# Recurrent attention stage: the queries' rotated halves go to TensorE unsummed, the keys are summed on VectorE, and the stage's steps stand in another order

## The chip, the cores and the metric

The program runs on one core of a Trainium2 chip. The metric is device time in microseconds (us) for one execution of the whole program; lower is better. Three runs of the kernel before gave 5869.11, 5871.00 and 5874.72 us, median 5871.0.

## What is computed

The reference is a decoder of four layers in float32 over x of 16 sequences, 128 positions and 256 features. Each layer has attention, a second attention and a feed-forward part. The change lies in the first part alone, a delta-rule recurrence with 8 heads of 64 and 8 modes per head. In short, for each sequence and head:

```
q, k = l2norm(x Wq), l2norm(x Wk);  v = x Wv;  beta, decay, gate from x
for each of 8 modes m: rotate q and k by the position times the mode's frequency
    rot(y) = y * cos + swap(y) * sin          (swap: the halves of 64 exchanged, one negated)
    S_t = decay_t * S_(t-1) + beta_t * k_t (v_t - k_t^T S_(t-1))      out_t += weight_m * q_t^T S_t
y = (gate * out) Wo;  x = layernorm(x + y)
```

## The kernel before, in words

`delta_stage` (L581) takes the 16 sequences one after the other. The recurrence over 128 positions is written in blocks of Q = 32: decayed products of keys with keys (they couple positions) and of keys with queries (they read the result out), the inverse of the coupling inside each block, and a solve over the four blocks. The 64 chains (8 heads by 8 modes) are cut in two halves of 32, and each half in four **packs** (2 heads by 4 modes). Partitions hold 4 modes by 32 positions.

Work by engine, in the order in which each engine takes it:

- VectorE. `rotate` (L1093) makes for a pack the two products of `rot` for the keys (j = 0) and for the queries (j = 1): `plain` (L1102) into `kq`, `swapped` (L1107) into `t1`, 128x512 each. `evacuate` (L1112) multiplies the pack's products in PSUM by the decays: two instructions for key by key (L1119), two for key by query (L1124). `invert` (L1128) inverts 32x32 triangles of all lanes with 60 instructions that each wait for the one before (L1150, L1151); it puts steps of `rotate` between them. `gated` (L1157), `sum_squares`, `clip`, `normalise` (L1178) and the layer norm serve the start of the next sequence and the end of the last.
- GpSimd. `add_halves` (L674, L679) adds `t1` to `kq`, 128x512, for keys and for queries, so twice per pack. `roots` (L668, L672) raises the sums of squares to the power -0.5, and `stage_x` copies x.
- TensorE. `prepare` (L794): two matmuls (L798) spread the log decays of the pack, then 64 small ones (L809) make both kinds of products, keys and queries of a block in turn. They wait for both sums of the pack (`rotated`) and for PSUM to be free (`outputs_ready`). `solve` (L814) does the couplings (L828, L834), the blocks' solutions (L847) and the readout (L857). `carrier` (L724) is a 1-column matmul that carries a wait.
- ScalarE. `exponentials` (L972, L977) turns log decays into decays, `diagonal` (L981, L985) copies the diagonal blocks for `invert`, and `solve` (L989) copies between the steps.

One turn of the loop (L896, L1253) is `part_b(g)` and `part_a(g + 1)`. **Part b** on TensorE is `solve` of half 0 and the four packs of half 0 of the next sequence. **Part a** is `solve` of half 1, pack 0 of half 1, `finish` (L865), `values` (L742, L790), pack 1, `pre_a` (x of the next sequence turned and projected, L750, L742), packs 2 and 3, and `pre_b` (the normalised keys and queries turned, L761, and swapped, L766; then the decays' tables, L770 to L781). VectorE's `part_a` (L1189) inverts half 0 and evacuates half 1; `part_b` (L1214) the other way round. Order and waits are all written by hand.

Of the kernel before, what the change touches and what calls it, by code (L numbers as in the profile page):

```python
# [21 lines left out]
ALU = mybir.AluOpType  # L22
# [558 lines left out]
def delta_stage(k):  # L581
# [18 lines left out]
    consts_ready tables_ready angles_ready reduced halves_ready rotated products_ready blocks_ready outputs_ready  # L600
# [50 lines left out]
    with nc.Block() as block:  # L651
# [6 lines left out]
        def _(pool):  # L658
# [15 lines left out]
            def add_halves(u, p):  # L674
                n = u * PACKS + p
                for j in range(2):
                    pool.wait_ge(s["halves_ready"], n * 2 + j + 1)
                    both = kq[:, p % 2, :, j, :]
                    pool.tensor_tensor(both, both, t1[:, j, :, :], ALU.add).then_inc(s["rotated"], 1)  # L679

            def part_a(g, first, more, more2):
                u = g * 2 + 1
                add_halves(u, 0)
                add_halves(u, 1)
                add_halves(u, 2)
                if not first:
                    norm.roots(pool, g - 1)
                if more:
                    roots(g + 1)
                if more2:  # L690
                    pool.wait_ge(s["low_written"], at_A(g) + 7)
                    stage_x(g + 2)
                add_halves(u, 3)

            def part_b(g):
                for p in range(PACKS):
                    add_halves(g * 2 + 2, p)
# [6 lines left out]
            for p in range(PACKS):  # L704
                add_halves(0, p)
            part_a(0, True, True, True)
            with pool.Fori(0, B - 3) as g:
                part_b(g)
                part_a(g + 1, False, True, True)
            part_b(B - 3)  # L710
            part_a(B - 2, False, True, False)
            part_b(B - 2)
# [4 lines left out]
        def _(pe):  # L717
# [38 lines left out]
            def pre_b(g, low):  # L756
# [7 lines left out]
                for j in range(2):  # L764
                    bank = low.bank()
                    nc.tensor.matmul(ps[:, bank, :], w.swap, qkT[:, j, :, :], start=True, stop=True  # L766
                                     ).then_inc(s["low_written"], 1)
                pe.wait_ge(s["logs_ready"], g + 1)
# [25 lines left out]
            def prepare(u, hf, p, low):  # L794
# [6 lines left out]
                if not (isinstance(n, int) and n < 1):  # L801
                    pe.wait_ge(s["outputs_ready"], n * 2)
                carrier(2)
                for q in range(NQ):
                    for j in range(2):
                        for m in range(4):
                            for hh in range(2):
                                rows = slice(hh * DK, (hh + 1) * DK)
                                mm = nc.tensor.matmul(ps[m * Q:(m + 1) * Q, 2 + 2 * hh + j, AT[q]:AT[q] + P - q * Q],  # L809
                                                      kq[rows, p % 2, m, 0, q * Q:(q + 1) * Q],  # L810
                                                      kq[rows, p % 2, m, j, q * Q:P], start=True, stop=True)
                mm.then_inc(s["products_ready"], 1)
# [55 lines left out]
            def part_a(g, first, more):  # L868
# [23 lines left out]
            pre_b(0, low)  # L892
# [13 lines left out]
        def _(act):  # L906
# [40 lines left out]
            def pre_b(g, low, diagonal=None):  # L947
                act.wait_ge(s["decays_clipped"], g + 1)
                nc.scalar.activation(logs, logs, ACT.Ln).then_inc(s["logs_ready"], 1)
                if not (isinstance(g, int) and g < 1):  # L950
                    act.wait_ge(s["halves_ready"], g * (HALVES * PACKS * 2))
# [4 lines left out]
                if diagonal:  # L956
                    diagonal()
# [2354 lines left out]
```

## Time and profile before

| | us |
|---|---|
| median of three runs | 5871.0 |
| the profiled execution, its own time | 5864.7 |
| its span, first to last instruction | 5862.8 |
| GpSimd's sums L679 (256), busy | 373.7 |
| VectorE's inverse L1150, busy | 381.3 |
| TensorE's products L809 (16384 matmul records), busy | 280.4 |

The clock granted to TensorE over the whole span is 0.791 of full speed. One record of the profile is one pass of a matmul, so a float32 matmul of L809 has two records; each record has a weight load beside it (PEld). "issue" as the reason of an idle time means that the engine waited for nothing that the profile shows. An instruction's duration goes on while it waits for a port.

### The profile page before, as it was taken

The page shows a single profiled execution, that of the slowest core. Times are in us where ns is not written, and L with a number is a line of the kernel's source. Part 1 is how long each engine was busy: PE and PEld are TensorE (multiplying, and loading weights), DVE is VectorE, ACT ScalarE, POOL GpSimd, SP SyncE. Part 2 cuts the span into 40 slices and gives each one's busy share as a digit, 9 for nine tenths or more (in the row PEclk, how much of TensorE's full clock was granted, in tenths as well). Part 3 has the DMA queues.
Part 4 walks back from the last instruction along what each step waited for, and adds up shares of the span by engine and source line. Part 5 has one row for each costly group of instructions (what it writes and reads, how often), then busy time and mean ns, then how long its engine had stood idle before and what let it go on. Part 6 is the DMA issues. An engine that isn't in the chain of part 4 may idle for free. (4 is left out here: it accounts for less than half of the span.)

```text
span 5862.8 us, 127205 instructions
## 1 busy us (share of the span) xinstructions
PE 4132.5 (70%) x52916; PEld 2838.7 (48%) x52916; DVE 3427.7 (58%) x7691; ACT 1529.9 (26%) x3081; POOL 985.0 (17%) x753
## 2 busy tenths in 40 slices
PE   2677777767777775667878646766854777877897
PEld 1455555555555543555555423434632455655454
DVE  6778777777877743115454556882445454444445
ACT  2333333333333311112222231111333222321111
POOL 1222221222221222113222100001100121211000
PEclk8788888788878887888887765556866887888999
DMA  0000000000000001640000000001000000000000
GB/s 36 3 3 3 3 3 3 3 3 3 3 3 3 3 23 37 231 170 9 0 29 11 15 0 4 1 1 40 0 6 0 10 0 25 7 1 6 14 19 25
DMA packets 26763, 111.26 MB, mean 19 GB/s; under 512 B 2407, under 2 KB 15742, under 8 KB 22270
## 3 DMA queue, kind: packets, MB, share of 16 engines
q1 hardware_dynamic: 24702, 99.57, 4.8%
q8 instruction: 390, 6.39, 0.4%
q0 software_dynamic: 1536, 4.20, 0.2%
q14 instruction: 135, 1.11, 0.1%
HBM read 93.53 MB, written 10.22 MB: 18 GB/s over the span
## 5 line engine op out<-in xcount | busy, mean ns | idle before, releaser
L679 POOL TENSOR_TENSOR arena<-arena 128x512 f32<-128x512 f32 x256 | 373.7, 1462 | 1296.8 <-DVE arena L1107 1296.8
L1150 DVE TENSOR_TENSOR arena<-weights,arena 128x30 f32<-128x30 f32 (+14 forms) x960 | 381.3, 397 | 33.2 <-DVE arena L1151 3.3
L144 POOL TENSOR_TENSOR arena<-arena,eps 128x4 f32<-128x4 f32 (+2 forms) x76 | 15.1, 199 | 2186.6 <-DVE arena L139 2186.6
L422 PE MATMUL psum<-ident,arena 128*128 128x128 f32 x1280 | 217.6, 325 | 212.6 <-ACT arena L493 212.6
L402 PE MATMUL psum<-arena 128*128 128x512 f32 x640 | 353.4, 685 | 16.8 <-ACT arena L482 11.2
L1151 DVE TENSOR_TENSOR arena<-arena 128x30 f32<-128x30 f32 (+14 forms) x960 | 317.6, 331 | 30.3
L414 PEld LDWEIGHTS psum<-arena 128*128 128x128 f32 x2048 | 280.8, 214 | 100.8 <-issue 59.7
L809 PE MATMUL psum<-arena 64*32 64x128 f32 (+2 forms) x16384 | 280.4, 286 | 50.5 <-issue 50.5
L300 POOL TENSOR_TENSOR arena<-arena,weights 128x1024 f32<-128x1024 f32 x128 | 242.5, 1902 | 405.1 <-PE psum L402 339.1
L977 ACT ACTIVATE arena<-psum,arena 128x128 f32<-128x128 f32 (+3 forms) x1024 | 240.2, 340 | 249.9 <-PE psum L798 246.7
L414 PE MATMUL psum<-arena 128*128 128x17 f32 x2048 | 272.9, 277 | 33.4 <-ACT arena L490 33.4
L1398 PE MATMUL psum<-arena 128*128 128x512 f32 x576 | 260.6, 598 | 50.5 <-DVE Y L1462 35.8
L422 PEld LDWEIGHTS psum<-ident,arena 128*128 128x128 f32 x1280 | 178.8, 171 | 234.8 <-ACT arena L493 234.6
L809 PEld LDWEIGHTS psum<-arena 64*32 64x32 f32 x16384 | 258.7, 126 | 61.3 <-issue 60.6
L724 PE MATMUL psum<-arena 128*128 128x1 bf16 x400 | 71.6, 179 | 281.8 <-ACT arena L993 98.9
L493 ACT ACTIVATE arena<-arena 128x1024 f32<-128x1024 f32 x160 | 169.7, 1061 | 349.4 <-DVE arena L549 348.3
L553 DVE RECIPROCAL arena<-psum 128x16 f32<-128x16 f32 x80 | 20.6, 258 | 384.1 <-PE psum L414 384.1
L1107 DVE TENSOR_TENSOR arena<-arena,Y 128x512 f32<-128x512 f32 x256 | 244.4, 955 | 0.0
L1119 DVE TENSOR_TENSOR arena<-psum,arena 128x320 f32<-128x320 f32 x256 | 113.6, 481 | 222.8 <-PE psum L809 219.1
L798 PE MATMUL psum<-arena 96*128 96x320 f32 x512 | 212.0, 529 | 44.7 <-ACT arena L970 21.6
L490 ACT COPY arena<-psum 128x1024 f32<-128x1024 f32 x160 | 162.1, 1013 | 307.8 <-PE psum L422 307.8
L724 PEld LDWEIGHTS psum<-arena 128*128 128x128 bf16 x400 | 40.5, 101 | 413.7 <-ACT arena L993 156.0
(457 smaller groups left out, 8678.5 us busy)
## 6 DMA issues: line engine op xcount, KB each, us to landing
arena<-in_experts_L_ffn SPq DMA_DIRECT2D x23, 2052.0 KB
arena<-in_ctxT SPq DMA_DIRECT2D x16, 512.0 KB, 3.4
arena<-in_experts_L_ffn SPq DMA_DIRECT2D x18, 384.0 KB, 3.0
weights<-in_w_L_ffn SPq DMA_DIRECT2D x1, 3072.0 KB, 9.9
weights<-in_w_L_attn SPq DMA_DIRECT2D x1, 2960.5 KB, 13.0
routed_x<-arena SPq DMA_DIRECT2D x1, 2944.0 KB, 16.5
routed_y<-arena SPq DMA_DIRECT2D x23, 128.0 KB, 1.7
weights<-in_w_L_ffn SPq DMA_DIRECT2D x1, 2753.0 KB, 10.2
```

What stands on the lines that cost most here:

```text
L300: pool.tensor_tensor(km[:, j % 2, :, :], bc(keys, 1, HH), bc(w.heads, 2, P), ALU.mult).then_inc(keys_spread, 1)
L402: mm = nc.tensor.matmul(out[:, b * 4:b * 4 + 4, :], qT[:, c, u * P:(u + 1) * P], km[:, at % 2, b * 4:b * 4 + 4, :], start=True, stop=True)
L414: mm = nc.tensor.matmul(o_psum[:, c * HH + h, :], pT[:, j % 2, h, :], v, start=True, stop=True)
L422: mm = nc.tensor.transpose(pt_psum[:, h, :], pr[:, j % 2, h, :], k.ident[:, :])
L679: pool.tensor_tensor(both, both, t1[:, j, :, :], ALU.add).then_inc(s["rotated"], 1)
L798: nc.tensor.matmul(ps[:, bank, 0:SPAN], pick[0:CHAINS + Q, hf * SLOTS + slot(p, hh), :], moving[0:CHAINS + Q, :], start=True, stop=True).t ...
L809: mm = nc.tensor.matmul(ps[m * Q:(m + 1) * Q, 2 + 2 * hh + j, AT[q]:AT[q] + P - q * Q], kq[rows, p % 2, m, 0, q * Q:(q + 1) * Q], kq[rows, ...
L977: a = nc.scalar.activation(LA[hf][:, t, 1, run], ps[:, bank, run], ACT.Exp, bias=bias[:, hf * SLOTS + t, q:q + 1])
L1107: dve.tensor_tensor(t1[:, j, :, :], bc(qkS[:, j, c, :], 1, 4), sin[:, c, modes4, :], ALU.mult).then_inc(s["halves_ready"], 1)
L1150: linked(dve.tensor_tensor(part, bc(lanes[:, j + 1:, j], 2, j), bc(inv[:, j, 0:j], 1, below), ALU.mult))
L1151: linked(dve.tensor_tensor(inv[:, j + 1:, 0:j], inv[:, j + 1:, 0:j], part, ALU.add))
L1398: mm = nc.tensor.matmul(ps[:, bank, :], W[s][name][:, c, f * P:(f + 1) * P], xT[:, g, c, :], start=(c == 0), stop=(c == C - 1))
```

## The change

The order on VectorE and TensorE, word for word from the built programs. The first place is one pack in the loop on TensorE, `prepare`. Before:

```order
L798 MATMUL psum<-arena 128x320
L800 ISA
L802 REGISTER_ALU
L724 MATMUL psum<-arena 128x1
L809 MATMUL psum<-arena 32x128 x16
L809 MATMUL psum<-arena 32x96 x16
L809 MATMUL psum<-arena 32x64 x16
L809 MATMUL psum<-arena 32x32 x16
```

The same place on TensorE in the change (L779 is L798 of before, L703 the carrier, L792 the products):

```order
L703 MATMUL psum<-arena 128x1
L792 MATMUL psum<-arena 32x128 x8
L792 MATMUL psum<-arena 32x96 x8
L792 MATMUL psum<-arena 32x64 x8
L792 MATMUL psum<-arena 32x32 x8
L784 REGISTER_ALU
L703 MATMUL psum<-arena 128x1
L792 MATMUL psum<-arena 32x128 x16
L792 MATMUL psum<-arena 32x96 x16
L792 MATMUL psum<-arena 32x64 x16
L792 MATMUL psum<-arena 32x32 x16
```

A pack has now 32 products of keys and then 64 of queries, with a second carrier between them: 96 in place of 64.

The second place is TensorE's part a, behind the projections of `values`. Before:

```order
L790 MATMUL psum<-arena,weights 128x128 x8
L735 REGISTER_ALU
L798 MATMUL psum<-arena 128x320
L735 REGISTER_ALU
L798 MATMUL psum<-arena 128x320
L800 ISA
L724 MATMUL psum<-arena 128x1
L809 MATMUL psum<-arena 32x128 x16
```

In the change, at the same place on TensorE (L771 is L790, L729 is L750, L721 is L742):

```order
L771 MATMUL psum<-arena,weights 128x128 x8
L726 REGISTER_ALU
L714 REGISTER_ALU
L729 MATMUL psum<-ident,arena 128x128 x2
L731 REGISTER_ALU
L714 REGISTER_ALU
L721 MATMUL psum<-weights,arena 128x512 x4
L714 REGISTER_ALU
L721 MATMUL psum<-weights,arena 128x128 x2
L714 REGISTER_ALU
L779 MATMUL psum<-arena 128x320
```

The next sequence's x is turned and projected ahead of pack 1. In the same way the turns and swaps (L761, L766; now L740, L745) stand ahead of pack 3, and only the tables behind it.

The third place is VectorE's `rotate` of one pack in the loop's part a. Before:

```order
L1102 TENSOR_TENSOR arena<-arena,weights 128x4x128
L1106 ISA
L1107 TENSOR_TENSOR arena<-arena,Y 128x512
L1102 TENSOR_TENSOR arena<-arena,weights 128x4x128
L1106 REGISTER_ALU
L1107 TENSOR_TENSOR arena<-arena,Y 128x512
```

In the change, at the same place on VectorE:

```order
L1120 TENSOR_TENSOR arena<-psum,arena 128x2x320
L1125 SCALAR_TENSOR_TENSOR arena<-psum,arena 128x320 x2
L1091 TENSOR_TENSOR arena<-arena,weights 128x4x128
L1095 ISA
L1096 TENSOR_TENSOR arena<-arena,Y 128x512
L1100 TENSOR_TENSOR arena<-arena,weights 128x4x128
L1103 REGISTER_ALU
L1104 TENSOR_TENSOR arena<-arena 128x4x128
L1108 TENSOR_TENSOR arena<-arena,Y 128x4x128
```

Five steps in place of four: L1104 sums the keys' halves, and the queries' swapped half (L1108) goes into `kq` of its own. The evacuation ahead of it is one instruction for both heads' keys (L1120) and two for the queries.

The core of the diff:

```
-    kq = A(2, 4, 2, P)
-    t1 = A(2, 4, P)
+    kq = A(2, 4, 3, P)
+    t1 = A(4, P)
...
-    inv, prod = A(Q, Q), A(Q * Q // 4)
+    prod = A(Q * Q // 4)
...
-            def add_halves(u, p):
-                n = u * PACKS + p
-                for j in range(2):
-                    pool.wait_ge(s["halves_ready"], n * 2 + j + 1)
-                    both = kq[:, p % 2, :, j, :]
-                    pool.tensor_tensor(both, both, t1[:, j, :, :], ALU.add).then_inc(s["rotated"], 1)
...
                 pe.wait_ge(s["rotated"], (n + 1) * 2)
...
+                for j, free, ready in ((0, "blocks_ready", "keys_ready"), (1, "outputs_ready", "queries_ready")):
+                    if not (isinstance(n, int) and n < 1):
+                        pe.wait_ge(s[free], n * 2 if j else n)
+                    carrier(2 + 2 * j)
+                    parts = (1, 2) if j else (0,)
+                    for q in range(NQ):
+                        for part in parts:
...
+                                                          kq[rows, p % 2, m, part, q * Q:P],
+                                                          start=(part == parts[0]), stop=(part == parts[-1]))
+                    mm.then_inc(s[ready], 1)
...
                 values(low)
-                prepare(u, 1, 1, low)
                 if more:
                     pre_a(g + 1, low)
+                prepare(u, 1, 1, low)
                 prepare(u, 1, 2, low)
+                if more:
+                    turns(g + 1, low)
                 prepare(u, 1, 3, low)
                 if more:
-                    pre_b(g + 1, low)
+                    tables(g + 1, low)
...
                 diagonal(u, 1, 0)
+                diagonal(u, 1, 1)
                 if more:
-                    pre_b(g + 1, low, lambda: diagonal(u, 1, 1))
-                else:
-                    diagonal(u, 1, 1)
+                    tables(g + 1, low)
...
+                def summed():
+                    dve.wait_ge(s["halves_ready"], n + 1)
+                    dve.tensor_tensor(kq[:, p % 2, :, 0, :], kq[:, p % 2, :, 0, :], t1[:, :, :], ALU.add
+                                      ).then_inc(s["rotated"], 1)
+
+                def swapped_queries():
+                    dve.tensor_tensor(kq[:, p % 2, :, 2, :], bc(qkS[:, 1, c, :], 1, 4), sin[:, c, modes4, :], ALU.mult
+                                      ).then_inc(s["rotated"], 1)
+
+                return [keys, swapped_keys, queries, summed, swapped_queries]
...
+                pair = L.rearrange("p (c h a) j t -> p c h a j t", c=2, h=2)[:, p // 2, :, p % 2, :, :]
+                kk = ps[:, 2:4, 0:SPAN]
+                dve.tensor_tensor(pair[:, :, 0, :], kk, pair[:, :, 1, :], ALU.mult).then_inc(s["blocks_ready"], 1)
...
-                linked(dve.tensor_copy(inv[:, :, :], lanes[:, :, :]))
-                linked(dve.memset(flat(inv)[:, 0:Q * Q:Q + 1], 1.0))
+                linked(dve.memset(flat(lanes)[:, 0:Q * Q:Q + 1], 1.0))
```

GpSimd's `add_halves` is gone with all its calls. The inverse is made in place in `lanes`, without the copy L1144. VectorE's `part_a` evacuates pack 1 behind `sum_squares` and `clip`, and runs `normalise` ahead of the evacuation of pack 2 and of the norm's last step.

## Rows read from the trace of the kernel before

**Rows 1.** Groups of instructions of the stage, 60 to 2060 us (count, busy, mean ns, idle before).

```profile
L679 POOL TENSOR_TENSOR arena<-arena 128x512 f32<-128x512 f32 x256 | 373.7, 1462 | 1296.8 <-DVE arena L1107 1296.8
...
L1107 DVE TENSOR_TENSOR arena<-arena,Y 128x512 f32<-128x512 f32 x256 | 244.4, 955 | 0.0
...
L1102 DVE TENSOR_TENSOR arena<-arena,weights 128x512 f32<-128x512 f32 x256 | 208.4, 814 | 5.4 <-ACT arena L955 5.4
...
L1178 DVE SCALAR_TENSOR_TENSOR arena<-arena 128x512 f32<-128x512 f32 x32 | 47.6, 1526 | 5.1 <-POOL arena L672 3.3
...
L1144 DVE COPY arena<-weights 128x1024 f32<-128x1024 f32 x32 | 22.0, 687 | 0.6
```

**Rows 2.** Windows of one turn: length, busy of PE, PEld, DVE, ACT, POOL; granted clock.

```profile
938.14:972.28 34.14, 26.19 (x854) 19.44 (x855) 32.09 (x72) 7.88 (x19) 5.66 (x4) 0.85 0.02 4
972.28:996.38 24.10, 14.74 (x467) 10.46 (x468) 17.86 (x30) 9.12 (x36) 7.47 (x5) 0.85 0.01 3
996.38:1026.68 30.30, 20.57 (x786) 15.61 (x784) 27.98 (x69) 5.42 (x15) 4.19 (x3) 0.89 0.02 4
1026.68:1064.36 37.68, 29.53 (x520) 20.38 (x520) 19.54 (x37) 20.64 (x51) 10.76 (x9) 0.77 0.01 2
```

**Rows 3.** Timeline of VectorE in both inversions: start, us, line, idle before and its end.

```profile
938.14 1.25 DVE L1143 STREAM_TRANSPOSE weights<-weights 128x1024 f32<-128x1024 f32 x1 [3.72 <-ACT weights L985]
...
946.02 1.77 DVE L1102 TENSOR_TENSOR arena<-arena,weights 128x512 f32<-128x512 f32 x1
...
1000.10 1.25 DVE L1150 TENSOR_TENSOR arena<-weights,arena 128x30 f32<-128x30 f32 x1
```

**Rows 4.** One line's instructions in the same turn: ns min/median/max, first and last start.

```profile
L1107 DVE TENSOR_TENSOR arena<-arena,Y x16: 675/682/1755, 942.5 to 1050.5; 128x512 f32<-128x512 f32 x16
```

**Rows 5.** Timeline of TensorE, end of part b's solve and its packs.

```profile
959.44 0.87 PE L828 MATMUL psum<-arena 32*32 32x64 f32 x47 [0.54 <-issue]
...
963.32 0.94 PE L847 MATMUL psum<-arena,weights 32*32 32x64 f32 x50 [0.64 <-issue]
...
965.06 4.28 PE L857 MATMUL psum<-arena 128*64 128x128 f32 x64
...
974.84 1.66 PE L809 MATMUL psum<-arena 64*32 64x128 f32 x127
978.77 0.19 PE L809 MATMUL psum<-arena 64*32 64x32 f32 x1 [2.27 <-issue]
...
981.15 2.22 PE L809 MATMUL psum<-arena 64*32 64x128 f32 x120
984.69 0.27 PE L809 MATMUL psum<-arena 64*32 64x32 f32 x8 [1.32 <-issue]
...
990.71 0.29 PE L809 MATMUL psum<-arena 64*32 64x32 f32 x15 [2.06 <-issue]
```

**Rows 6.** The page, DMA queues: packets, MB, share.

```profile
q8 instruction: 390, 6.39, 0.4%
```

**Rows 7.** Timeline of TensorE in part a behind `gated`, one turn earlier.

```profile
900.91 3.51 PE L865 MATMUL psum<-weights,arena 128*128 128x256 f32 x8 [6.97 <-DVE arena L1159]
...
907.75 0.70 PE L798 MATMUL psum<-arena 96*128 96x320 f32 x2
...
910.70 2.50 PE L809 MATMUL psum<-arena 64*32 64x128 f32 x128
...
914.35 4.14 PE L742 MATMUL psum<-weights,arena 128*128 128x512 f32 x12 [0.54 <-ACT arena L939]
...
921.94 2.58 PE L809 MATMUL psum<-arena 64*32 64x128 f32 x128
...
929.80 0.18 PE L724 MATMUL psum<-arena 128*128 128x1 bf16 x1 [4.01 <-POOL arena L679]
...
932.42 1.97 PE L761 MATMUL psum<-ident,arena 128*128 128x128 f32 x8
934.21 2.22 PE L766 MATMUL psum<-arena,weights 128*128 128x512 f32 x4
```

More of the change, by code:

```diff
@@ L690, in part_a @@
                 if more2:
-                    pool.wait_ge(s["low_written"], at_A(g) + 7)
+                    pool.wait_ge(s["low_written"], at_A(g) + 5)
                     stage_x(g + 2)
[L693 to L697, printed above, removed]
             pool.wait_ge(s["consts_ready"], 1)
@@ L800, in prepare @@
                 pe.wait_ge(s["rotated"], (n + 1) * 2)
[L801 to L812, printed above, removed]
+                for j, free, ready in ((0, "blocks_ready", "keys_ready"), (1, "outputs_ready", "queries_ready")):
[5 more added lines that the diff above has]
+                        for part in parts:
+                            for m in range(4):
+                                for hh in range(2):
+                                    rows = slice(hh * DK, (hh + 1) * DK)
+                                    mm = nc.tensor.matmul(ps[m * Q:(m + 1) * Q, 2 + 2 * j + hh,
+                                                             AT[q]:AT[q] + P - q * Q],
+                                                          kq[rows, p % 2, m, 0, q * Q:(q + 1) * Q],
+                                                          kq[rows, p % 2, m, part, q * Q:P],
+                                                          start=(part == parts[0]), stop=(part == parts[-1]))
+                    mm.then_inc(s[ready], 1)
             def solve(g, hf):
@@ L891, in _ @@
             pre_a(0, low)
-            pre_b(0, low)
+            turns(0, low)
+            tables(0, low)
             for p in range(PACKS):
@@ L1026, in _ @@
             pre_a(0, low)
-            pre_b(0, low)
+            turns(0, low)
+            tables(0, low)
             for p in range(PACKS):
@@ L1110, in rotate, with keys, swapped_keys @@
-                return steps
+                def keys():
+                    if turned is not None:
+                        dve.wait_ge(s["low_taken"], turned)
+                    dve.tensor_tensor(kq[:, p % 2, :, 0, :], bc(qkT[:, 0, c, :], 1, 4), cos[:, c, modes4, :], ALU.mult)
+                def swapped_keys():
+                    if not (isinstance(n, int) and n < 1):
+                        dve.wait_ge(s["rotated"], n * 2 - 1)
+                    dve.tensor_tensor(t1[:, :, :], bc(qkS[:, 0, c, :], 1, 4), sin[:, c, modes4, :], ALU.mult
+                                      ).then_inc(s["halves_ready"], 1)
@@ L1149, in invert @@
                     part = prod[:, 0:below * j].rearrange("p (a b) -> p a b", b=j)
[L1150 to L1151 removed]
+                    linked(dve.tensor_tensor(part, bc(lanes[:, j + 1:, j], 2, j), bc(lanes[:, j, 0:j], 1, below), ALU.mult))
+                    linked(dve.tensor_tensor(lanes[:, j + 1:, 0:j], lanes[:, j + 1:, 0:j], part, ALU.add))
                 assert not between
```

82 lines of the change are left out of this document (30 added, 52 removed).

## The prediction

> **What bounds the kernel now.** I read the groups of instructions of the stage first. GpSimd's 256 sums (L679) take 1.46 us each and VectorE's instructions beside them are long: L1107 has a mean of 0.955 us, L1102 of 0.814 [rows 1]. Then one line alone: of 16 L1107 in a turn the median is 0.682 us and the longest 1.755 [rows 4]. So most run at 0.68 and some at 1.75, and the timeline shows these where a sum of GpSimd runs: 1.77 us for an L1102, 1.25 for an L1150 of 30 columns that elsewhere takes 0.2 [rows 3]. A collision costs VectorE about 1.07 us.
>
> Next the windows of one turn, cut where VectorE changes work: inversion of part b to `gated` (34.14 us), evacuation of part b (24.10), inversion of part a (30.30), evacuation of part a (37.68), together 126.2 us [rows 2]. VectorE is busy for 94% and 92% of the inversions, but for 74% and 52% of the evacuations. There it waits for TensorE. The change touches this stage alone, so I count one turn, and 15.5 of them (16 sequences, with a short first and last).
>
> Last, why TensorE is late in part b. Its packs stop in the middle of a run of equal matmuls, with "issue" as the reason: 2.27, 1.32 and 2.06 us [rows 5]. Between two such stops lie always 126 records: 1 + 4 (L798) + 1 (carrier) + 120, then 8 + 4 + 1 + 113. A record has a weight load, so that is 252 instructions, and the page has a queue that brings instructions in packets of 6.39 MB / 390 = 16.4 KB [rows 6]. I read it so: TensorE runs out of instructions and waits for the next packet. Where nothing else holds it up, packets are 963.32 - 959.44 = 3.9 us apart; in the packs, with a wait for VectorE between them, 5.9 and 6.0 us [rows 5]. A packet's records need only 126 x 13.1 ns = 1.7 us (1.66 us for 127) [rows 5].
>
> **The change part by part**, per turn.
>
> *GpSimd's sums go.* VectorE's collisions go with them. In the inversion of part b four instructions are of the long kind (one stands in [rows 3]): -4.3. In that of part a two of L1150: -2.1. In the evacuations some more, beside waits, L1178 among them (mean 1.526 against 0.68) [rows 1].
>
> *The sum comes to VectorE.* Eight packs, a fifth 128x512 instruction each. Started back to back, one takes some 0.6 us of VectorE (0.68 less the overlap): two more steps in the inversion of part b, +1.2, one in that of part a, +0.6, five in the evacuations, +3.0, the most of it under waits for TensorE.
>
> *The copy L1144 goes*, twice 0.69 [rows 1]: -0.7 in each inversion. One evacuation of 640 columns for two of 320, the memset and the order of `clip` and `sum_squares` I cost at nothing: they move 0.1 us and stand before waits.
>
> *Inversion of part a*: -2.1 - 0.7 + 0.6 = -2.2. VectorE is the bound here, TensorE waits 6.97 us at its end [rows 7].
>
> *Inversion of part b*: VectorE alone would save 4.3 + 0.7 - 1.2 = 3.8. But `gated` needs TensorE's readout, L857, which ends at 965.06 + 4.28 = 969.34, 2.9 before `gated` at 972.28 [rows 2, 5]. And the solve starts later against the inversion: the tables (1.3 us) now stand behind pack 3, and then come the loop's jump and the solve. I take -1.5, between -2.9 and 0.
>
> *Packs of part b.* Now 192 records, 4 of L798 and 2 carriers: 198, four times 792, that is 6.3 packets. One is there: 1.7 us; the other 5.3 take 3.9 each, 20.6. Last product 22.3 us after the readout, where before it was 991.0 - 972.3 = 18.7 after `gated`: +3.6. Behind it VectorE's next rotation has no collision but a fifth step, -1.1 + 0.6, and pack 0's part of the work had lain before `gated` (nearly 3 us of it; that is why the gap between readout and `gated` is spent first): of these I leave -0.8. So part b together: -1.5 + 3.6 - 0.5 - 0.8 = +0.8. Price of a packet between 1.7 (hidden) and 5.9; I take 3.9, the row with nothing else in it, since the new second wait (keys free PSUM ahead of queries) lets TensorE run on.
>
> *Evacuation of part a* is a chain over TensorE, which I put together anew from [rows 7]: from `gated` 0.5; `finish` and `values`, 900.91 to 907.75, 6.8; x turned and copied, 913.20 to 914.35, 1.2; projections, ScalarE's part and the decays, 914.35 to 921.94, 7.6; packs 1 and 2 with 192 records between 13.1 and 20.2 ns (2.58 us for 128), 2.5 to 3.9, I take 3.2 each; decays between them 1.4; turns and swaps, 932.42 to 936.4, with ScalarE 4.3; decays 1.4; pack 3 3.2 and its evacuation 1.0. Sum 33.8. Gone are the 4.01 us in which pack 3 waited for GpSimd's sum [rows 7] and the 3.72 in which the inversion waited for ScalarE's diagonals behind the turns [rows 3]. Packets: three packs are 4.7 of them, some 2.7 of which can't be there in time; I add 2.0. So 35.8 against 37.68 [rows 2]: -1.9, bounds -3.9 (all there) and +1.5 (5.9 us each). And L865 ran 3.51 us for 8 records of 256, the lower level of the clock (1.2 GHz), behind its 6.97 us of waiting [rows 7]; its wait shrinks by the 2.2 of the inversion and the 1.0 of the longer pack 0. Half of 1.7 us: -0.8.
>
> **Sum**: +0.8 - 2.2 - 1.9 - 0.8 = -4.1 us per turn, times 15.5 is -64 us. The profiled execution took 5864.7 us; the median of the runs, 5871.0, is 6 above. So 5801 on its clock and **5807** as a median.
>
> **A rule of the Trainium skill against the row.** The row shows stops of 2.27, 1.32 and 2.06 us, 126 records apart [rows 5]. In "Runtime: NRT & Kernel Launch", section on instruction fetch mechanics, the Trainium skill says that the sequencer fetches the next 16 KiB page while it works on the current one, and that crossing the boundary is "mostly hidden". By that rule the added instructions would cost their execution alone, the first rival below; the trace disagrees, since what stops the packs comes at just this spacing.
>
> **The rivals.**
>
> *The added packets are hidden* (chance 0.10). Then part b follows VectorE and the readout: -2.9, the packs nothing; part a -2.2 - 3.9. Together -9.0, 5731 us. For it: no such stops stand in part a's rows [rows 7]. Against it: part b's three.
>
> *TensorE's instructions become the bound* (0.12, slower). Place: the packs, 5.3 packets beyond the first in part b and 2.7 in part a, 8.0 together. Each 1 us above 3.9 adds 8.0 us, so from 4.4 us per packet the gain is gone. Half way to the 5.9 seen between the stops of part b, 4.9 us, the turn is 8.0 - 4.1 = 3.9 longer: 5931. For it: each pack still waits for VectorE in two places. Against it: the 3.9 of the solve, where TensorE waits for ScalarE as well.
>
> *Nothing is left* (0.08, within 0.2%). The solve of part b starts 4 us later against the inversion than before (tables, then the jump, L834), VectorE waits at `gated` for it, and -1.5 becomes +2.6: 5871.
>
> *The change doesn't do what it says*: the order shows 96 products per pack and no sum on GpSimd, so I give it nothing.
>
> **The numbers.** The forecast has 0.70; with the first rival 0.80 is faster by over 0.2% (12 us, about what a measurement of this kernel tells from no change), 0.08 within it, 0.12 slower. The range holds the forecast's own bounds, the hidden packets below and the zero case's near side above: 5735 to 5868. Left out are the slower rival and a part of the zero case.
>
> **What would show it.** VectorE's 128x512 instructions all near 0.68 us; windows of 28 us for part a's inversion and some 35 for its evacuation; part b as long as before, with two stops "issue" per pack or so, 126 records apart, near 2 us each; q8 with about 64 packets more (128 packs x 128 instructions more / 252). The forecast is wrong if part b grows by over 4 us, if part a's packs show stops above 2 us each, or if VectorE waits over 3 us at `gated` in part b.

## The result and the profile after

Four executions of the changed kernel gave 5778.6 to 5792.0 us, median **5778.9**; four of the kernel before, in the same comparison, had a median of 5872.9. The ratio is 0.9845, with a 95% interval of 0.9828 to 0.9862: 94 us less. The forecast was 5807 us, 64 less, within 5735 to 5868.

| | before | after |
|---|---|---|
| span of the profiled execution | 5862.8 | 5776.9 |
| GpSimd busy, whole span | 985.0 | 602.4 |
| VectorE busy, whole span | 3427.7 | 3284.6 |
| TensorE's products, stops "issue" before them (groups) | 50.5 | 119.7 |
| clock granted to TensorE, share of full speed | 0.791 | 0.819 |

The groups of instructions after, 60 to 1975 us, which answer to [rows 1] (count, busy, mean ns, idle before with its end):

```profile
L792 PE MATMUL psum<-arena 64*32 64x128 f32 (+3 forms) x24576 | 375.8, 243 | 120.5 <-issue 119.7
...
L1125 DVE SCALAR_TENSOR_TENSOR arena<-psum,arena 128x320 f32<-128x320 f32 x256 | 129.2, 546 | 124.2 <-PE psum L792 118.6
...
L1120 DVE TENSOR_TENSOR arena<-psum,arena 128x640 f32<-128x640 f32 x128 | 105.0, 820 | 144.5 <-ACT arena L965 109.6 <-PE psum L792 33.1
...
L1100 DVE TENSOR_TENSOR arena<-arena,weights 128x512 f32<-128x512 f32 x128 | 87.8, 686 | 0.0
L1108 DVE TENSOR_TENSOR arena<-arena,Y 128x512 f32<-128x512 f32 x128 | 87.7, 685 | 0.0
...
L1178 DVE SCALAR_TENSOR_TENSOR arena<-arena 128x512 f32<-128x512 f32 x32 | 20.6, 684 | 3.3 <-POOL arena L672 3.3
```

The 128x512 instructions have now one length, 0.68 to 0.69 us, where L1107 had a mean of 0.955 and L1178 of 1.526. What VectorE waits for stands in the other rows: TensorE's queries (118.6 us) and ScalarE's decays (109.6).

The windows of one turn, cut at the same places as [rows 2]:

```profile
893.47:924.39 30.92, 22.80 (x721) 16.93 (x722) 28.30 (x73) 4.78 (x9) 0.00 (x0) 0.83 0.02 4
924.39:949.68 25.29, 19.66 (x860) 15.41 (x861) 16.52 (x28) 11.85 (x43) 0.00 (x0) 0.96 0.02 5
949.68:977.44 27.76, 21.07 (x851) 15.88 (x849) 25.54 (x69) 5.49 (x15) 0.00 (x0) 0.97 0.02 4
977.44:1016.15 38.71, 30.69 (x715) 20.43 (x715) 17.82 (x35) 18.10 (x49) 4.24 (x5) 0.91 0.01 3
```

Both inversions are shorter. The evacuation of part b is longer, that of part a no shorter. One turn can stand 2 us off another, so the table below has means: the same four pieces, taken from the starts of the inversion's first transpose (L1143, now L1144) and of `gated` (L1159 in both) in each trace, over the 14 turns between the second sequence and the last.

| run | median us | inversion b | evacuation b | inversion a | evacuation a | turn |
|---|---|---|---|---|---|---|
| before | 5872.9 | 34.1 | 23.3 | 30.3 | 37.8 | 125.4 |
| **after** | 5778.9 | 30.2 | 25.3 | 27.8 | 37.4 | 120.7 |
| e1_products_64 | 5753.2 | 31.9 | 21.9 | 27.8 | 37.2 | 118.8 |
| e2_products_128 | 5996.8 | 30.4 | 33.9 | 27.8 | 42.2 | 134.1 |
| e11_narrow_products | 6000.2 | 30.8 | 34.1 | 27.8 | 41.6 | 134.3 |
| e3_old_order | 5794.2 | 30.8 | 26.2 | 27.8 | 36.5 | 121.2 |
| e4_before_no_sums | 5742.4 | 30.4 | 24.2 | 28.0 | 35.5 | 118.1 |
| e5_keys_on_gpsimd | 5821.8 | 31.5 | 25.0 | 28.2 | 38.0 | 122.7 |
| e6_queries_on_vector | 5821.0 | 32.1 | 24.1 | 28.1 | 38.2 | 122.5 |
| e7_before_in_place | 5857.3 | 33.4 | 23.8 | 29.4 | 38.0 | 124.6 |
| e8_late_queries | 5734.1 | 32.2 | 22.7 | 28.4 | 34.2 | 117.5 |
| e9_values_first | 5685.2 | 30.4 | 25.4 | 27.8 | 30.6 | 114.2 |
| e10_both | 5672.3 | 32.1 | 22.7 | 28.4 | 30.2 | 113.3 |
| e12_unrolled | 5669.4 | 31.7 | 22.1 | 28.4 | 31.5 | 113.7 |

One execution of e11_narrow_products took 14692.5 us at a granted clock of 0.572 and bears on no reading; without it that run's median is 5999.4 us.

A turn is 4.7 us shorter. Fourteen of them are 65.7 us, but the distance from the first inversion to the last shrank by 86.6 (1928.8 to 1842.2). Most of the rest lies in the first turn, which took 119.3 us and takes 100.3. Its part a has no `solve` and no `finish`. The first turn's windows before, from one inversion's first transpose to the next, columns as above:

```profile
123.83:185.17 61.34, 30.02 (x642) 19.88 (x643) 44.95 (x100) 20.60 (x51) 14.64 (x10) 0.68 0.00 1
185.17:243.15 57.98, 41.86 (x1320) 31.26 (x1321) 49.84 (x101) 17.08 (x53) 13.16 (x9) 0.72 0.01 3
```

and after:

```profile
123.95:172.67 48.72, 29.26 (x834) 21.34 (x834) 41.54 (x97) 16.65 (x47) 3.61 (x3) 0.81 0.01 2
172.67:224.28 51.61, 39.95 (x1646) 30.16 (x1646) 44.57 (x102) 17.85 (x54) 0.00 (x0) 0.97 0.02 4
```

Part b's packs on TensorE after, which answer to [rows 5] (start, us, line, idle before and its end):

```profile
930.72 0.28 PE L792 MATMUL psum<-arena 64*32 64x32 f32 x10 [0.44 <-issue]
930.93 0.18 PE L703 MATMUL psum<-arena 128*128 128x1 bf16 x1
931.04 1.53 PE L792 MATMUL psum<-arena 64*32 64x128 f32 x117
934.20 0.28 PE L792 MATMUL psum<-arena 64*32 64x32 f32 x11 [1.62 <-issue]
...
938.03 1.06 PE L792 MATMUL psum<-arena 64*32 64x96 f32 x83 [0.51 <-issue]
...
941.51 0.39 PE L792 MATMUL psum<-arena 64*32 64x64 f32 x26 [0.47 <-issue]
...
945.26 0.34 PE L792 MATMUL psum<-arena 64*32 64x32 f32 x27 [1.90 <-issue]
```

Between two stops lie 126 to 128 records (10 + 1 + 117 in the first gap). The stops are 3.48, 3.83, 3.48 and 3.75 us apart, 3.6 on average, where before they were 5.9 and 6.0. The packs now run at about the pace that the solve had shown (3.9). The page counts 454 packets of instructions for 390 [rows 6]:

```profile
q8 instruction: 454, 7.44, 0.5%
```

### The profile page after: what moved, and what is told of

Same layout as the page of the kernel before. It is cut to its first block and busy times, and to the rows that moved or that the text cites. A ratio compares the mean times of both kernels' runs of the same rounds, so it can differ in the third digit from the quotient of the medians.

```text
span 5776.9 us, 143172 instructions
## 1 busy us (share of the span) xinstructions
PE 4179.0 (72%) x61228; PEld 2889.5 (50%) x61236; DVE 3284.6 (57%) x7659; ACT 1490.3 (26%) x3051; POOL 602.4 (10%) x497
## 5 line engine op out<-in xcount | busy, mean ns | idle before, releaser
L792 PE MATMUL psum<-arena 64*32 64x128 f32 (+3 forms) x24576 | 375.8, 243 | 120.5 <-issue 119.7
L792 PEld LDWEIGHTS psum<-arena 64*32 64x32 f32 x24576 | 323.2, 108 | 180.8 <-issue 178.2
L402 PE MATMUL psum<-arena 128*128 128x512 f32 x640 | 356.2, 690 | 16.8 <-ACT arena L482 11.2
L1151 DVE TENSOR_TENSOR weights<-weights,arena 128x30 f32<-128x30 f32 (+14 forms) x960 | 318.0, 331 | 32.1 <-DVE arena L1150 2.9
L1150 DVE TENSOR_TENSOR arena<-weights 128x30 f32<-128x30 f32 (+14 forms) x960 | 317.7, 331 | 29.3
L414 PEld LDWEIGHTS psum<-arena 128*128 128x128 f32 x2048 | 282.9, 216 | 101.7 <-issue 60.9
L414 PE MATMUL psum<-arena 128*128 128x17 f32 x2048 | 274.8, 278 | 33.4 <-ACT arena L490 33.4
L1398 PE MATMUL psum<-arena 128*128 128x512 f32 x576 | 260.6, 598 | 50.5 <-DVE Y L1462 35.8
L813 PEld LDWEIGHTS psum<-arena 32*32 32x32 f32 x12288 | 188.1, 108 | 87.3 <-issue 85.9
L813 PE MATMUL psum<-arena 32*32 32x64 f32 x12288 | 219.0, 220 | 12.0 <-issue 11.6
L819 PE MATMUL psum<-arena 128*128 128x512 f32 x256 | 182.4, 801 | 50.0 <-issue 47.3
L402 PEld LDWEIGHTS psum<-arena 128*128 128x128 f32 x640 | 133.0, 227 | 136.8 <-issue 110.7
L1125 DVE SCALAR_TENSOR_TENSOR arena<-psum,arena 128x320 f32<-128x320 f32 x256 | 129.2, 546 | 124.2 <-PE psum L792 118.6
L1398 PEld LDWEIGHTS psum<-arena 128*128 128x128 f32 x576 | 109.5, 191 | 165.6 <-issue 109.0
```

The costliest lines, as they stand in the source:

```text
L402: mm = nc.tensor.matmul(out[:, b * 4:b * 4 + 4, :], qT[:, c, u * P:(u + 1) * P], km[:, at % 2, b * 4:b * 4 + 4, :], start=True, stop=True)
L414: mm = nc.tensor.matmul(o_psum[:, c * HH + h, :], pT[:, j % 2, h, :], v, start=True, stop=True)
L792: mm = nc.tensor.matmul(ps[m * Q:(m + 1) * Q, 2 + 2 * j + hh, AT[q]:AT[q] + P - q * Q], kq[rows, p % 2, m, 0, q * Q:(q + 1) * Q], kq[rows, ...
L813: mm = nc.tensor.matmul(ps[rows, 6, t * DK:(t + 1) * DK], Lu[rows, t, 0, col:col + Q], Wn[rows, t, by, :], start=False, stop=(by == q - 1 ...
L819: mm = nc.tensor.matmul(ps[:, 6, :], repeat[:, q, :], bc(slots, 2, 2), start=True, stop=(q == 0))
L1150: linked(dve.tensor_tensor(part, bc(lanes[:, j + 1:, j], 2, j), bc(lanes[:, j, 0:j], 1, below), ALU.mult))
```

## The experiments

In what was expected, theory P is that of the prediction: packets of instructions set the length of part b's packs.

**What a product costs, by itself and by its instructions.** Three runs with 64, 128 and again 128 products per pack, the last with added products of 8 columns in place of 32 to 128. The edits, each to the change:

```
e1: -  parts = (1, 2) if j else (0,)      +  parts = (1,) if j else (0,)
e2: -  parts = (1, 2) if j else (0,)      +  parts = (1, 2, 2) if j else (0,)
e11:   as e2, the added product with q * Q:q * Q + 8 in place of q * Q:P
```

> The change with the queries' second product left out of TensorE (64 products per pack again, 32 fewer); the result leaves out sin * swap(q), VectorE still makes it. Theory P (packets of instructions set the length of part b's packs, 3.9 us per 126 records): 64 records fewer are half a packet, 2.0 us per pack, of which part b gives back some 5 of 8 before VectorE binds and part a some 3: about -8 us per turn, 5655 us; q8 back to about 390 packets. Rival X (only their execution counts, 13.1 ns a record): 0.84 us per pack, -3.4 in part b and at most -2.5 in part a: 5690 to 5730 us. Rival V (VectorE hides them): under -1 us per turn, 5765 or more.

> The change with the queries' second product made twice, so 128 products per pack, 64 records more per pack (the result has that half twice). Theory P: +2.0 us per pack in part b and +1 to +2 in three packs of part a: +11 to +13 us per turn, 5950 to 5980 us, with stops 'issue' in the packs summing to more than twice those of the change (120 us before L792) and about 64 packets more in q8. Rival X: the records' execution alone, +0.84 us per pack, +3.4 and +2.5 per turn: 5870 us. Rival V: under +1 us per turn, 5795 or less.

> As the run with 128 products per pack (5996.8 us), but the 32 added products of each pack are 8 columns wide in place of 128 to 32, so they bring the same number of instructions and nearly no work (the result has sin * swap(q) twice in 8 of a block's columns). Theory P (the count of instructions, by their packets, is what costs): the evacuation of part b stays near 33.9 us as with the wide ones (33 to 34), q8 near 519 packets, 5960 to 5995 us. Rival X (the products' own execution and the clock): most of the 218 us that the wide ones cost goes away, the evacuation of part b near 26 to 28 us, 5800 to 5860 us.

Measured: 5753.2, 5996.8 and 6000.2 us, against 5778.9 for the change. The 32 products that the change adds cost 26 us, the next 32 cost 218, and 32 of 8 columns cost 221. The window of one evacuation of part b with the wide ones:

```profile
878.78:912.62 33.84, 24.84 (x1103) 19.36 (x1105) 16.48 (x29) 11.10 (x42) 0.00 (x0) 0.84 0.02 4
```

the same with the narrow ones:

```profile
1019.46:1054.15 34.69, 25.14 (x1099) 19.61 (x1102) 16.48 (x29) 11.31 (x42) 0.00 (x0) 0.82 0.02 4
```

the page's queue with the narrow ones (the wide ones have the same 519):

```profile
q8 instruction: 519, 8.50, 0.6%
```

and TensorE's timeline with the narrow ones:

```profile
1022.94 1.47 PE L793 MATMUL psum<-arena 64*32 64x96 f32 x128 [0.42 <-issue]
1026.69 0.25 PE L793 MATMUL psum<-arena 64*32 64x32 f32 x3 [2.27 <-issue]
...
1045.95 1.59 PE L793 MATMUL psum<-arena 64*32 64x128 f32 x128 [0.49 <-issue]
1049.70 0.45 PE L793 MATMUL psum<-arena 64*32 64x8 f32 x27 [2.15 <-issue]
```

with the wide ones, from the same place as the third of these lines:

```profile
1038.53 1.61 PE L792 MATMUL psum<-arena 64*32 64x128 f32 x128 [0.48 <-issue]
```

As many added instructions with a small part of the columns cost the same: what is paid for is the count. The narrow run alone does not tell packets from execution, since a narrow record takes TensorE nearly as long: 128 records, a third of them narrow, take 1.59 us and 128 wide ones 1.61, and the window has 25.14 us busy for 24.84. Two other numbers do. The 64 added records cost 2.1 us per pack in part b (8.5 over four), where theory P had 2.0 and their execution at 13.1 ns is 0.84. And the stops with the narrow ones are 3.75 us and 128 records apart at a granted clock of 0.82, hardly more than in the change at 0.96, so the lower clock explains little of it. The runs lie 17 and 5 us above theory P's ranges, and its size is right for these 64 records.

It is not right for the 64 records that the change itself adds. There part b's evacuation grew by 3.4, or 0.85 per pack, which is their execution, and part b's inversion gave 1.7 of it back. With 64 products VectorE waits at `gated` for the readout (L1159, 32 of them):

```profile
L1159 DVE TENSOR_TENSOR arena<-psum,arena 128x256 f32<-128x256 f32 x32 | 13.2, 414 | 49.1 <-PE psum L842 49.1
```

Of the 49.1 us, 25.3 stand before the last `gated` of the program, which has such a wait in every run; the rest is 1.5 us in nearly every turn. The change has 0.9 us in all before its first 30. TensorE's solve starts 6.3 us behind the inversion's first transpose, where in the change it is 3.4 (means of the 14 turns). So the next solve came too late for the shorter packs to be worth their full length. Of the three theories for that run none had the time: X came nearest from one side (5690 to 5730), V from the other (5765 or more).

**What the sums on GpSimd cost.** The kernel before, its sums cut to one column:

```
-                    both = kq[:, p % 2, :, j, :]
-                    pool.tensor_tensor(both, both, t1[:, j, :, :], ALU.add)
+                    both = kq[:, p % 2, 0:1, j, 0:1]
+                    pool.tensor_tensor(both, both, t1[:, j, 0:1, 0:1], ALU.add)
```

> The kernel before with GpSimd's sums cut from 128x512 to one column, so that the sum of the halves is left out of the result but for that column; all waits and the order as before. Theory C (a sum of GpSimd makes the VectorE instruction beside it 1.07 us longer): all 128x512 instructions of L1102 and L1107 near 0.68 us, inversion of part b -2.9 to -4.3, inversion of part a -2.1, evacuation of part a -3 to -4 with the wait for L679 gone, of part b -1: 9 to 11 us per turn, 5700 to 5730 us. Rival N (the long instructions have another cause, such as the order or PSUM): the long ones stay near 1.75 us, only the wait of 4.01 us goes, 5810 us.

And the change with the keys' sum given back to GpSimd (`summed` leaves VectorE's list, GpSimd has `add_halves` again for j = 0):

> The change with the keys' sum back on GpSimd (128 sums in place of 256), the queries unsummed on TensorE as in the change; VectorE has four steps per pack. Theory C: each of the eight sums per turn falls on a VectorE instruction and makes it 1.07 us longer, where VectorE's own step would take 0.60: in the inversions, three sums, +0.5 each, +1.4; in the evacuations the sum also comes later to TensorE (1.46 + 0.3 us behind the last step, against 0.68), +1 per pack that TensorE waits for, 2 to 3 of them: +3 to +5 us per turn, 5825 to 5855 us. Rival L (one step less on VectorE outweighs it): 5740 to 5770 us.

Measured: 5742.4 us, 133 below the 5875.2 of the kernel before in the same comparison, and 5821.8, 43 above the change. One line's instructions in the first of the two (ns min/median/max):

```profile
L1107 DVE TENSOR_TENSOR arena<-arena,Y x256: 675/687/708, 93.6 to 1921.4; 128x512 f32<-128x512 f32 x128
```

and in the second, with GpSimd's sum:

```profile
L1122 DVE TENSOR_TENSOR arena<-arena,Y x128: 677/1755/1775, 94.6 to 1996.1; 128x512 f32<-128x512 f32 x128
...
L678 POOL TENSOR_TENSOR arena<-arena x128: 1284/1653/3710, 94.2 to 1995.6; 128x512 f32<-128x512 f32 x128
```

Without the sums no instruction of L1107 is longer than 0.71 us, where [rows 4] had 1.755. With one sum per pack 1.755 is the median of the line beside it. Theory C stands: the collision is the cause, 1.07 us each. The sums of the expectations were too high: 133 us and 7.3 per turn for 9 to 11 (part b's evacuation gave nothing), and 43 us and 2.0 per turn for 3 to 5. The Trainium skill says in "SBUF — State Buffer", section "Who interferes with whom", that a VectorE instruction with two SBUF inputs contends with a GpSimd instruction that reads SBUF; these three rows agree.

**What one step on VectorE costs.** The change with the queries summed on VectorE too, so six steps and 64 products:

```
-                return [keys, swapped_keys, queries, summed, swapped_queries]
+                return [keys, swapped_keys, queries, summed, swapped_queries, summed_queries]
```

> The change with the queries' halves summed on VectorE too: six steps per pack, 64 products per pack on TensorE; the same result. Theory P (a pack's 32 added products cost up to 2.0 us of packets in part b, a VectorE step 0.60): part b's packs some 3 us shorter, the inversions 3 x 0.60 = 1.8 longer, part a's packs about 1 shorter: -2 us per turn, 5735 to 5760 us. Rival X (the products cost 0.84 us per pack and partly lie under VectorE's waits): the step costs more than it saves, +1 us or more per turn, 5790 to 5810 us.

Measured: 5821.0 us. Against the run with 64 products, which has one step fewer and the same products, that is 68 us for the sixth step: 3.7 per turn. Three of its eight stand in part b's evacuation and cost 2.1, two in part a's and cost 0.9, the one in part a's inversion costs 0.4 and the two in part b's 0.2, since with 64 products VectorE waits 1.5 us for the readout there and the added steps fill that wait. Rival X was right and still too low. A step costs its 0.60 us or more only in part b's evacuation (0.7).

**The copy and the order.** The kernel before with the inverse made in place alone (`inv` replaced by `lanes`, L1144 gone), and the change with part a's steps in the order of before:

> The kernel before with the inverse made in place, so the copy L1144 gone, and nothing else changed. By the prediction's step: -0.7 us in each inversion where VectorE is the bound, so -0.7 in part a and -0.7 in part b (the readout ends 2.9 us ahead of gated): -1.4 us per turn, 5850 us. Rival: the inversion's rotate steps then meet GpSimd's sums at other places and TensorE's next pack comes no earlier, so nothing: 5866 to 5873 us.

> The change's products and sums, but the steps of part a in the order of the kernel before (pack 1 ahead of the next x, turns and tables behind pack 3, diagonals of the second half behind the turns). Theory O (the new order is worth the 3.72 us in which the inversion waited for ScalarE's diagonals, and little else, since the 4.01 us of waiting for GpSimd's sum is gone in either order): +3 to +5 us per turn in part a, 5825 to 5855 us; part b as in the change. Rival C (all of the gain comes from VectorE's collisions with GpSimd, the order is worth nothing): 5770 to 5790 us. Rival G (the order is all of the gain): 5860 us or more.

Measured: 5857.3 us, 0.9969 of before (0.9957 to 0.9982), 18 us or 0.8 per turn in the means for the 1.4 of the expectation. The old order: 5794.2 us, 15 above the change. A steady turn is 0.5 us longer, from part b (+0.9 and +0.6 us); part a's evacuation is 0.9 *shorter* in the old order. That makes 7 us in 14 turns. Another 7.4 lie in the first turn (107.7 us for 100.3). The first transpose then waits for ScalarE's diagonals (59.3 us over 32), where in the change it waits 25.9 for "issue" alone. So theory O (+3 to +5 per turn) was wrong by a factor of six or more, and rival C nearly right: in the steady turns the order is worth half a microsecond, and in the first turn 7.4.

**Where VectorE waits in the change.** Its timeline in the turn shown above, the waits alone:

```profile
924.39 0.43 DVE L1159 TENSOR_TENSOR arena<-psum,arena 128x256 f32<-128x256 f32 x1 [0.65 <-PE psum L842]
...
945.75 1.01 DVE L1125 SCALAR_TENSOR_TENSOR arena<-psum,arena 128x320 f32<-128x320 f32 x2 [2.79 <-PE psum L792]
...
993.99 1.22 DVE L1164 TENSOR_REDUCE arena<-arena 128x16 f32<-128x1024 f32 x1 [10.24 <-ACT arena L931]
...
1013.14 1.01 DVE L1125 SCALAR_TENSOR_TENSOR arena<-psum,arena 128x320 f32<-128x320 f32 x2 [2.46 <-PE psum L792]
1016.15 1.25 DVE L1144 STREAM_TRANSPOSE weights<-weights 128x1024 f32<-128x1024 f32 x1 [2.00 <-issue]
```

Two of these kinds can be tried by a move alone. The 2.79 and 2.46 us are waits for the last pack's queries, which the inversion does not need:

```
-                    evacuate(u, 0, 3, e + 6)
+                    evacuate_keys(u, 0, 3, e + 6)
...
-                invert(g * 2, ch, rotate(u, 1, 1))
+                invert(g * 2, ch, [lambda: evacuate_queries(g * 2, 0, 3)] + rotate(u, 1, 1))
```

(and the same for the other half). The 10.24 us are the chain that begins at `gated`:

```
                 prepare(u, 1, 0, low)
+                values(low)
                 if not first:
                     finish(g - 1)
-                values(low)
```

> The change with one thing moved on VectorE: in the last pack of each half only the keys are evacuated ahead of the inversion (it needs nothing else), the queries' two instructions L1125 go behind the inversion's first transpose. Theory Q (the 2.8 and 2.5 us in which VectorE waits for the products of the last pack's queries stand on the path that sets the turn): -3 us in part b and -3 in part a, 6 us per turn, 5685 us, and the readout becomes what gated waits for. Rival R (TensorE's solve, which follows its own packs, tables and jump, sets gated anyway): gated waits for the readout, -1 us per turn or less, 5765 us.

> The change with values (the projections L721 and L771) ahead of finish on TensorE, in the time in which it waits for gated; nothing else moved. Theory S (part a's evacuation is a chain from gated over finish, values, the turned x and the projections, 977.88 to 993.97 in the trace of the change, and VectorE waits 10.24 us for its end): the 4.2 us of values leave the chain, and ScalarE's sigmoid with its table load starts with gated and not 7.3 us behind it: -4 to -6 us per turn, all in the evacuation of part a, 5690 to 5720 us. Rival P (behind that chain come the packs, whose packets then bind): -1 us per turn or less, 5765 us.

> Values ahead of finish and the last pack's queries evacuated behind the inversion's transpose, together. Theory: the two lie on different stretches (evacuation of part a; end of both evacuations), so they add: -3 for the late queries (measured alone) and -4 to -6: 5640 to 5680 us. Rival (the readout becomes the bound of both halves once VectorE comes earlier): less than the larger of the two alone, 5690 us or more.

Measured: 5734.1, 5685.2 and 5672.3 us. The late queries took 2.7 and 3.2 us from the two evacuations and gave 2.0 and 0.6 back to the inversions. Both inversions now hold the two moved instructions, and in part b's `gated` waits 1.2 us per turn for the readout besides: half of theory Q, half of rival R. Values ahead of `finish` took 6.8 us from part a's evacuation and moved no other piece by over 0.2, theory S and a little beyond its 4 to 6. The window of one evacuation of part a in that run:

```profile
941.27:972.32 31.05, 25.09 (x710) 17.59 (x708) 17.84 (x36) 18.11 (x49) 4.25 (x5) 1.00 0.01 3
```

and what is left in it of the wait of 10.24 us:

```profile
950.22 1.22 DVE L1164 TENSOR_REDUCE arena<-arena 128x16 f32<-128x1024 f32 x1 [2.63 <-ACT arena L931]
```

TensorE's clock, 0.91 in that window of the change, is 1.00: the engine now has `values` to do ahead of `gated`. Together they gave 13 us beyond the better one, against some 45 if they added. So 5672.3 lies within the 5640 to 5680 of the expectation and still the two do not add. The result, 0.9653 of the kernel before (0.9637 to 0.9669), computes the same function and is 107 us below the change.

**The jump of TensorE's loop.** The last run takes that kernel and writes the loop's body twice:

```
-            with pe.Fori(0, B - 2) as g:
-                part_b(g, True)
-                part_a(g + 1, False, True)
+            with pe.Fori(0, (B - 2) // 2) as h:
+                for g in (h * 2, h * 2 + 1):
+                    part_b(g, True)
+                    part_a(g + 1, False, True)
```

> Both rearrangements of the run before (5672.3 us) and TensorE's loop body written out twice, so that 7 jumps in place of 14 stand ahead of part b's first L819. Theory J (the stop of 3.5 us 'issue' there is the jump, and behind it the solve and the readout set gated in part b): half of the stops gone, the inversion of part b 1.5 us shorter on average, 5645 to 5655 us. Rival (instead of the jump a packet is waited for at the same place, since the two stops have one cause): 5668 to 5676 us.

Measured: 5669.4 us, 3 below, within what such a measurement can tell. The groups of the products and of the solve's first matmuls with the body written twice:

```profile
L792 PE MATMUL psum<-arena 64*32 64x64 f32 (+3 forms) x24576 | 378.1, 245 | 135.1 <-issue 134.6
L819 PE MATMUL psum<-arena 128*128 128x512 f32 x256 | 170.0, 751 | 24.5 <-issue 21.6 <-DVE arena L1167 2.8
```

and in the kernel that it was made from:

```profile
L792 PE MATMUL psum<-arena 64*32 64x128 f32 (+3 forms) x24576 | 377.1, 244 | 110.6 <-issue 109.5
L819 PE MATMUL psum<-arena 128*128 128x512 f32 x256 | 180.3, 793 | 50.5 <-issue 49.4 <-DVE arena L1166 1.0
```

The stops ahead of L819 fell by 27.8 us and those in the packs grew by 25.1. A stop of 3.4 to 4.0 us stands behind the loop's jump 13 times with the body written once and 6 times (3.3 to 3.8 us) with it written twice, as often as the loop jumps back. The rival had the time right. The Trainium skill, "Runtime: NRT & Kernel Launch", section on instruction fetch mechanics, says that a taken branch whose target is outside the current window of two pages causes an instruction-fetch stall, and that this is a reason to unroll. Here a stall at the jump is seen; that its cause is this fetch is not shown, and unrolling moved it without making the sum less.

## Why the prediction was right, and where it was not

*Collisions* (-4.3 and -2.1 in the inversions, priced at 1.07 each from [rows 3, 4]): right, by the run without sums and the run with one sum.

*Inversion of part a*, -2.2: measured -2.5, and about 28 us as said. VectorE is the bound there: 27.8 to 28.4 in every run without GpSimd's 256 sums, whatever TensorE does.

*Inversion of part b*, -1.5: measured -3.8. This is exactly what was worked out for VectorE alone (4.3 + 0.7 - 1.2). The step that failed is the cut from 3.8 to 1.5, the readout as the next bound. The first matmul of TensorE's solve, and the readout after, in the turns shown (938.14 and 893.47 are the inversion's first transpose):

```profile
941.40 1.96 PE L834 MATMUL psum<-arena 128*128 128x512 f32 x2 [3.44 <-issue]
```

```profile
897.15 2.07 PE L819 MATMUL psum<-arena 128*128 128x512 f32 x2 [3.89 <-issue]
...
920.07 4.28 PE L842 MATMUL psum<-arena 128*64 128x128 f32 x64
```

Two things were mis-sized. The 2.9 us between the readout and `gated` are those of one turn; over the 14 turns before they are 4.7 on average (2.8 to 9.6). And the solve was to start later against the inversion, but it starts 3.4 us behind the first transpose where it had been 3.2 (means), so the readout ends as early as before, 29.0 us behind the transpose for 29.4. The readout is the next bound, but just reached: in the change `gated` waits for it in two of its first 30 places, 0.65 us in the turn shown.

```profile
L1159 DVE TENSOR_TENSOR arena<-psum,arena 128x256 f32<-128x256 f32 x30 | 12.0, 400 | 0.9 <-PE psum L842 0.9
```

With 64 products (e1) and with the late queries (e8), where the inversion starts earlier against TensorE's solve, this piece grew back by 1.7 and 2.0.

*Packs of part b*, +3.6 with -0.5 and -0.8 behind it, so +2.3: measured +2.1. The size is right, and the stops "issue" are there, 126 to 128 records apart. In the turn shown the last product ends 21.2 us behind `gated`, where I had 22.3: the price of a packet was taken as 3.9 and is 3.6. There are five stops over the four packs and not two per pack, and they are shorter than the 2 us each that I expected, 0.44 to 1.90. That packets are the reason for the +2.1 itself is not shown: taking the 32 added products away again gave 0.85 us per pack, no more than their execution. The rule of the Trainium skill that crossing a page is mostly hidden would have made the packs cost their execution; but five stops stand in four packs of the turn shown, 4.9 us together, and 64 records beyond the change cost 2.1 us per pack for 0.84 of execution, so the measurement decides against it here.

*Evacuation of part a*, -1.9, and -0.8 for the clock: measured -0.4. This is the term that failed. TensorE's timeline of the turn after, in the places that my chain named:

```profile
977.88 3.22 PE L850 MATMUL psum<-weights,arena 128*128 128x256 f32 x8 [3.55 <-DVE arena L1159]
...
987.45 5.84 PE L721 MATMUL psum<-weights,arena 128*128 128x512 f32 x12 [2.17 <-ACT arena L927]
...
995.28 0.94 PE L792 MATMUL psum<-arena 64*32 64x128 f32 x64
...
1004.00 1.09 PE L740 MATMUL psum<-ident,arena 128*128 128x128 f32 x8 [0.95 <-DVE arena L1178]
```

The products of pack 1 start 17.8 us behind `gated` (977.44), where my chain had 0.5 + 6.8 + 1.2 + 7.6 = 16.1. Of the 1.7 between them ScalarE has 1.4: from the turned x (984.90) to its projections (987.45) it is 2.6 us for the 1.2. Its timeline there:

```profile
985.17 1.28 ACT L958 ACT_TABLE_LOAD   x1 [1.26 <-PE psum L771]
986.46 0.60 ACT L958 ACTIVATE arena<-psum 128x512 f32<-128x512 f32 x1
986.96 0.37 ACT L927 COPY arena<-psum 128x256 f32<-128x256 f32 x1
```

x's copy (L927) now stands directly behind the gate's sigmoid (L958) and its table load, and TensorE waits 2.17 us for it, where in [rows 7] it waited 0.54. And behind the last pack I had its evacuation as the end; in fact VectorE then stops 2.00 us at what must be its own loop's jump: such a stop stands there 13 times, 1.96 to 2.06 us each and 25.9 together, as often as the loop jumps back. Before it had lain hidden in the 3.72 us of waiting for the diagonals [rows 3]. The added packets were priced right: from pack 1's products to the turns it is 8.7 us for 7.8, and pack 3's products take 4.4 for 3.2, together the 2.0 that I had put down. L850 took 3.22 us against 3.51: of the 0.8 for the clock 0.3 are seen there. The upper bound of the term, +1.5, left these 2.0 out; with them it is +3.5.

So per turn -4.7 for -4.1, from -3.8 -2.5 +2.1 -0.4 for -1.5 -2.2 +2.3 -2.7: two errors of opposite sign, each of 2.3 us. That the turn came out within 0.6 us is luck.

*The number of turns.* Counting 15.5 equal ones was the largest error, half of the distance from -64 to -94. The 14 steady turns give 65.7 for 57; the first gives 19.0 where it was counted at 4.1. In it the next sequence's x stood behind pack 1, which waits 21.8 us for VectorE, and now stands ahead of it. VectorE's three longest waits between the first two transposes, 7.01, 3.91 and 3.41 us before, became 4.18 and 0.68. The run in the old order has 7.4 of the 19.0 back; how the rest divides is open. Some 8 us between the spans' difference (85.9) and that of the medians are spread of the runs.

*The rivals.* Hidden packets, 5731: refuted by the stops and the narrow products. Packets as the bound: not reached, at 3.6 us per packet, but with 64 more records a pack the same place cost +218 us over the change. Nothing left: no. Its mechanism, the wait for the readout, is there only once something else in part b gets shorter.

*The parts by runs of their own*, all in us of the program: without sums -133, no copy -18, order -15, one more VectorE step +68, 32 products per pack +26. They add to -72 for a change that measured -94, so about 20 us are interplay (the step's price was taken in a kernel without collisions, the sums' in one without the step). The reading holds all the same: the gain is the sums' departure from GpSimd. Half of it is paid for the fifth step on VectorE, if that costs what the sixth did, and the queries' way over TensorE costs 26 where a sixth step costs 68.

Still open: why stops of 0.6 to 1.6 us remain in part b's packs with 64 products, where they are 4.2 to 4.8 us apart and so slower than the 3.6 us apart seen in the change. No run separated that.

## What to carry to other kernels

Price an instruction on the engine that waits for it, not where it is short: the same 0.68 us step cost 0.1 to 0.4 us per pack between the inversion's links and 0.5 to 0.7 in the evacuations, ahead of TensorE's packs. Where TensorE runs many small matmuls, count its instructions as well as its columns, and look for stops "issue" at an even spacing; a matmul of 8 columns cost as much here as one of 32 to 128. And look at what stands first behind a join: work that does not depend on it (here `values`) belongs ahead of the wait, and that was worth as much as the whole change, 94 us. Last, read a slack such as that between readout and `gated` over all turns, not from one: here it was 2.9 us in the turn shown and 4.7 on average.

## What was not expected of the hardware

- 32 matmuls of 8 columns more per pack cost 221 us of the program, 32 of 32 to 128 columns 218: no difference within the spread of the runs.
- The pace of packets in dense packs was 3.5 to 3.8 us for 126 to 128 matmul records, each with its weight load; in the kernel before, with a wait for VectorE between them, it was 5.9 and 6.0.
- Halving the number of jumps in TensorE's loop took 27.8 us of stops from one line and gave 25.1 to another.
